# A layer norm taken chunk by chunk, and a K/V loop that empties its banks with two engines

## The reference

```python
n = layernorm(x)                                # no scale, no shift
Q, K, V = n @ Wq, n @ Wk, n @ Wv
Qf, Kf = elu(Q) + 1, elu(K) + 1                 # elu(z)+1 = max(z,0) + exp(min(z,0))
KV = einsum('lm,ln->mn', Kf, V); K1 = Kf.sum(0) # for each head
x = x + ((Qf @ KV) / (Qf @ K1 + eps)) @ Wo      # linear attention
y = layernorm(x)
y = y + mla(rmsnorm(y))                         # causal softmax attention, latent of 512
x = x + y + moe(rmsnorm(y))                     # 8 experts, top 2, hidden 2048 (all computed)
```

## Time and profile before

| | us |
|---|---|
| median of 3 runs | 3589.64 (3584.74 to 3591.18) |
| the profiled execution, its time | 3570.58 |
| its span, slowest core (core 6) | 3568.7 |
| spans of all cores | 3548.9 to 3568.7 |
| TensorE matmul busy | 2762.1 (77% of the span) |
| VectorE, ScalarE, POOL busy | 819.2, 721.4, 364.5 |
| mean granted TensorE clock, all cores | 0.886 to 0.889 |

### The profile page before, as it was taken

How to read it: one execution, slowest core, us unless ns; L and a number is a source line. 1 busy time by engine, 2 the same in 40 slices (tenths; PEclk the granted TensorE clock), 3 DMA queues, 4 the chain that set the end, 5 groups by cost and what they waited for, 6 DMA issues and landing times.

```text
span 3568.7 us, 36830 instructions; the slowest of 8 cores (3548.9 to 3568.7 us)
## 1 busy us (share of the span) xinstructions
PE 2762.1 (77%) x13813; PEld 1240.7 (35%) x14080; DVE 819.2 (23%) x1585; ACT 721.4 (20%) x809; POOL 364.5 (10%) x375
## 2 busy tenths in 40 slices
PE   1678554894555666657999989999999899999997
PEld 1333221442222222223444434444444344444443
DVE  4325444355333232230110011001101110011011
ACT  2001100103352535632001101110111011101110
POOL 0113100000101000002001101110111011101110
PEclk9888776895666767878999999999999999999999
DMA  8001003001000000009246443652464536525641
GB/s 180 1 1 26 0 1 48 1 4 21 1 1 0 1 1 1 1 1 104 24 51 71 42 66 35 71 62 23 57 71 37 70 36 71 59 22 61 71 80 51
DMA packets 297853, 135.97 MB, mean 38 GB/s; under 512 B 268880, under 2 KB 269904, under 8 KB 297680
## 3 DMA queue, kind: packets, MB, share of 16 engines
q0 software_dynamic: 292432, 116.69, 28.3%
q1 hardware_dynamic: 5248, 16.91, 1.5%
HBM read 241.73 MB, written 8.39 MB: 70 GB/s over the span
## 4 chain that ended last, share of the span: by engine, by line
PE 66%; DVE 14%; ACT 6%; issue 5%; DMA 5%; another core or an unknown queue 1%; DVEq 1%; ACTq 0%; POOL 0%; SPq 0%; POOLq 0%
PE PS L966 24%; PE PSQ L938 22%; ACT PTb L727 5%; PE PSQ L287 4%; DMA WSb<-w 3%; PE PSQ L716 3%; DVE PTb L737 3%; DVE accT L976 3%; PE PSQ L398 2%; PE PST L202 2%; PE PS L699 2%; PE PS L786 2%; PE PSQ L353 2%; PE PSQ L557 2%; DMA accT<-x 1%
## 5 line engine op out<-in xcount | busy, mean ns | idle before, releaser
L938 PE MATMUL PSQ<-N,WSb 128*128 128x512 bf16 x4013 | 897.2, 383 | 42.6 <-DMA WSb<-w 37.1
L966 PE MATMUL PS<-N 128*128 128x512 bf16 x2758 | 624.1, 379 | 63.8 <-DVE accT L976 61.0
L976 DVE SCALAR_TENSOR_TENSOR accT<-PS,gts,accT 128x512 f32<-128x512 f32 x256 | 192.1, 751 | 1739.2 <-PE PS L966 1693.6
L938 PEld LDWEIGHTS PSQ<-N,WSb 128*128 128x128 bf16 x4096 | 403.5, 99 | 533.5 <-issue 60.7
L947 ACT ACTIVATE N<-PSQ 128x1024 bf16<-128x1024 f32 x256 | 261.9, 1023 | 1604.7 <-PE PSQ L938 1604.7
L966 PEld LDWEIGHTS PS<-N 128*128 128x128 bf16 x2816 | 270.5, 98 | 408.6 <-issue 92.6
L727 ACT ACTIVATE PTb<-PSQ 128x1024 bf16<-128x1024 f32 x320 | 327.4, 1023 | 225.1 <-PE PSQ L716 209.7
L151 POOL DMA_DIRECT2D WSb<-w x256 | 223.8, 874 | 1209.3 <-PE PSQ L938 1206.1
L966 PE MATMUL PS<-A,N 128*128 128x512 bf16 x1257 | 287.6, 379 | 37.4 <-DVE accT L976 36.2
L699 PE MATMUL PS<-N,PTb 128*128 128x65 bf16 x2176 | 146.7, 218 | 212.5 <-DVE PTb L737 158.4
L716 PE MATMUL PSQ<-qpad,N 128*128 128x512 bf16 x587 | 244.4, 523 | 12.7 <-issue 7.9
(11 more groups left out here) (128 smaller groups left out, 1206.1 us busy)
## 6 DMA issues: line engine op xcount, KB each, us to landing
WSb<-w POOLq DMA_DIRECT2D x256, 256.0 KB, 4.7
N<-w POOLq DMA_DIRECT2D x11, 2048.0 KB, 14.5
A<-w POOLq DMA_DIRECT2D x5, 2048.0 KB, 14.6
accT<-x SPq DMA_DIRECT2D x4, 2048.0 KB, 34.1
out<-accT SPq DMA_DIRECT2D x2, 4096.0 KB, 12.9
N<-aWk POOLq DMA_DIRECT2D x1, 2048.0 KB, 34.7
N<-aWv POOLq DMA_DIRECT2D x1, 2048.0 KB, 56.9
A<-aWq POOLq DMA_DIRECT2D x1, 2048.0 KB, 67.8
```

The lines of the kernel that those rows point to most:

```text
L938: st=(kc == 0), sp=(kc == KD - 1): e_.matmul(out=QB[bb], lhsT=w1slot[sl][:, kk * 128:(kk + 1) * 128], rhs=N1v[:, kk, g * 1024 + hf * 512:g ...
L966: st=(kh == 0), sp=(kh == KH - 1): e_.matmul(out=YEB[pp][:, 0:512], lhsT=N2a[:, kk * 1024 + t_ * 128:kk * 1024 + t_ * 128 + 128], rhs=w2a[ ...
L976: tst = b.emit("v", lambda e_, pp=pair[half], d=dstp, tt_=qt, ee=e: e_.scalar_tensor_tensor(out=d, in0=YEB[pp][:, 0:512], scalar=gts.ap()[ ...
```

## The change

Two places are changed. In the layer norm the three loops over 16 tiles become one loop over the four chunks of x: sums and squares of four tiles, the small instructions on 4 columns of `st`, then normalisation and transposition of those four tiles. The fourth tile of a chunk is transposed and copied behind the first normalisation of the next chunk. In the K/V loop max and min are taken by halves of 512 columns (one bank each), the copy of V goes from VectorE to ScalarE, ahead of the exponent, and the banks' tokens follow: bank 0 is free after the first min, bank 1 after the second, banks 2 and 3 after ScalarE's copy. VectorE's wait for POOL's addition of the round before (`scr_guard[0]`) now stands ahead of the first max.

```diff
-    tsq = None
-    for t in range(NT):
-        acc_t = accT.ap()[:, t * 1024:(t + 1) * 1024]
-        b.wait("v", tok_xc[t // 4])
-        b.wait("s", tok_xc[t // 4])
...
     pend_tr = None
-    for t in range(NT):
...
+    for c in range(4):
+        lo = 4 * c
+        b.wait("v", tok_xc[c])
+        b.wait("s", tok_xc[c])
+        tsq = None
+        for t in range(lo, lo + 4):
+            acc_t = accT.ap()[:, t * 1024:(t + 1) * 1024]
+            b.emit("v", lambda e, a=acc_t, tt=t: e.reduce_sum(out=st[:, 16 + tt:17 + tt], in_=a, axis=AX.X))
+            tsq = b.emit("s", lambda e, a=acc_t, tt=t: e.activation(
+                out=scrF.ap(), in_=a, func=AF.Square, accum_out=st[:, 32 + tt:33 + tt]), inc="s")
+        b.wait("v", tsq)
+        b.emit("v", lambda e, l=lo: e.tensor_scalar_mul(out=st[:, 16 + l:20 + l], in0=st[:, 16 + l:20 + l], scalar1=1.0 / 1024))
...
+        b.wait("s", tv)
+        tsd = b.emit("s", lambda e, l=lo: e.activation(out=st[:, 32 + l:36 + l], in_=st[:, 32 + l:36 + l], func=AF.Sqrt, bias=EPS_LN), inc="s")
+        b.wait("v", tsd)
+        b.emit("v", lambda e, l=lo: e.reciprocal(out=st[:, 32 + l:36 + l], in_=st[:, 32 + l:36 + l]))
+        for t in range(lo, lo + 4):
...
+            b.wait("v", slot_guard[t % 2])
+            ta = b.emit("v", lambda e, a=acc_t, sl=slot, tt=t: e.tensor_scalar(
+                out=sl, in0=a, scalar1=st[:, 16 + tt:17 + tt], scalar2=st[:, 32 + tt:33 + tt],
+                op0=ALU.subtract, op1=ALU.mult), inc="v")
+            if pend_tr is not None:
+                ev, mm = transpose_tile(*pend_tr[0:3])
...
         b.wait("v", kf_slot_free[sl])
-        b.wait("v", v_slot_free[sl])
         kpsum = PSQ.ap()[:, 0:1024]
-        b.emit("v", lambda e, kp=kpsum, d=kf: e.tensor_scalar_max(out=d, in0=kp, scalar1=0.0))
         b.wait("v", scr_guard[0])
-        tmin = b.emit("v", lambda e, kp=kpsum: e.tensor_scalar_min(out=scrF.ap(), in0=kp, scalar1=0.0), inc="v")
+        b.emit("v", lambda e, kp=kpsum, d=kf: e.tensor_scalar_max(out=d[:, 0:512], in0=kp[:, 0:512], scalar1=0.0))
+        tmin0 = b.emit("v", lambda e, kp=kpsum: e.tensor_scalar_min(out=scrF.ap()[:, 0:512], in0=kp[:, 0:512], scalar1=0.0), inc="v")
+        b.emit("v", lambda e, kp=kpsum, d=kf: e.tensor_scalar_max(out=d[:, 512:1024], in0=kp[:, 512:1024], scalar1=0.0))
+        tmin = b.emit("v", lambda e, kp=kpsum: e.tensor_scalar_min(out=scrF.ap()[:, 512:1024], in0=kp[:, 512:1024], scalar1=0.0), inc="v")
+        vdst = vp.rearrange("p (h c) -> p h c", c=65)[:, :, 0:64]
+        vsrc = PSQ.ap()[:, 1024:2048].rearrange("p (h c) -> p h c", c=64)
+        b.wait("s", tok_kv)
+        b.wait("s", v_slot_free[sl])
+        tv = b.emit("s", lambda e, d=vdst, s_=vsrc: e.activation(out=d, in_=s_, func=AF.Copy), inc="s")
         b.wait("s", tmin)
         b.wait("s", scr_guard[0])
         te = b.emit("s", lambda e: e.activation(out=scrF.ap(), in_=scrF.ap(), func=AF.Exp), inc="s")
-        vdst = vp.rearrange("p (h c) -> p h c", c=65)[:, :, 0:64]
-        vsrc = PSQ.ap()[:, 1024:2048].rearrange("p (h c) -> p h c", c=64)
-        tv = b.emit("v", lambda e, d=vdst, s_=vsrc: e.tensor_copy(out=d, in_=s_), inc="v")
-        bank_free[0] = bank_free[1] = tmin
+        bank_free[0] = tmin0
+        bank_free[1] = tmin
         bank_free[2] = bank_free[3] = tv
         b.wait("g", te)
-        b.wait("g", tv)
```

More of the change, by code:

```diff
@@ L236, in build @@
-    pend_tr = None
-    for t in range(NT):
[L238 to L247, removed]
+    pend_tr = None
@@ new lines, in build @@
+    for c in range(4):
[10 more added lines that the diff above has]
+        b.emit("v", lambda e, l=lo: e.tensor_scalar_mul(out=st[:, 16 + l:20 + l], in0=st[:, 16 + l:20 + l], scalar1=1.0 / 1024))
+        b.emit("v", lambda e, l=lo: e.tensor_scalar_mul(out=st[:, 32 + l:36 + l], in0=st[:, 32 + l:36 + l], scalar1=1.0 / 1024))
+        b.emit("v", lambda e, l=lo: e.tensor_mul(out=st[:, l:l + 4], in0=st[:, 16 + l:20 + l], in1=st[:, 16 + l:20 + l]))
+        tv = b.emit("v", lambda e, l=lo: e.tensor_sub(out=st[:, 32 + l:36 + l], in0=st[:, 32 + l:36 + l], in1=st[:, l:l + 4]), inc="v")
+        b.wait("s", tv)
[3 more added lines that the diff above has]
+        for t in range(lo, lo + 4):
+            acc_t = accT.ap()[:, t * 1024:(t + 1) * 1024]
+            slot = stg1.ap()[:, (t % 2) * 1024:(t % 2) * 1024 + 1024]
+            b.wait("v", slot_guard[t % 2])
[4 more added lines that the diff above has]
+                ev, mm = transpose_tile(*pend_tr[0:3])
+                slot_guard[pend_tr[3] % 2] = mm
+            pend_tr = (slot, N1v[:, 0:8, t * 128:(t + 1) * 128], [ta], t)
```

## The result

The changed kernel took 3551.26 us (median of 10 runs) beside 3587.63 us for the kernel before (10 runs): 36.4 us less, ratio 0.9897 with a 95% interval of 0.9876 to 0.9919. The forecast was 3554 us, 35.3 us less.

What follows compares the result with a forecast made beforehand. The prediction took the kernel as mostly TensorE-bound, with gains possible only at the start and in the K/V loop. 18.5 + 11.8 + 5 = 35.3 us off 3589.6 gave 3554 us, range 3540 to 3573.

Steps and rivals of the forecast that it cites:

- The start: Program start to first projection matmul: layer norm by chunks brings that matmul to 80.0 instead of 98.47, 18.5 us less.
- More than 18.5 isn't there: Layer norm at the start: upper bound of 18.5 us on the gain, because VectorE's queue is full.
- The weights: DMA at the start: Wv still lands near 59.9 us, 19 us before it is wanted, despite the moved normalisations.
- Rival C: Start: weights stand still under the moved VectorE work, so the time is 3590 us, no change; chance 0.03.
- The loop's wait: K/V loop: TensorE restarts 3.24 instead of 4.04 us after the first max, 12.0 us in 15 restarts, 11.8 with the tail.
- rival E: K/V loop: ScalarE's copy into steps of 65 is slow and TensorE waits for it, 3618 us at 7 us; chance 0.04.
- That bank 0 is given back early is worth nothing: K/V loop: early release of bank 0 gains nothing, as TensorE asks for all four banks before its first matmul.
- The clock: K/V loop: TensorE's bursts shorten with less idle time, 5 us less, between +14.6 and -25.4.
- 22% of 25.4: K/V loop: idle shrinks 22%, so that share of the 25.4 us from all bursts at 2.4 GHz, rounded down to 5.
- all like the last burst of 9.57 us: K/V loop: the clock term's bad bound, every TensorE burst as long as the last, 14.6 us more.
- rival D: K/V loop: the clock stays up throughout, gaining the whole 25.4 us, for a time of 3534 us; chance 0.11.
- Rival F: Expert stage: both gains are given back where TensorE already waits for weights, time 3590 us; chance 0.04.

Runs made afterwards that it cites:

- e1: Kernel before with only the layer norm by chunks, its K/V loop unchanged; ratio 0.9957 to the kernel before.
- e6: Changed kernel with ScalarE instead of VectorE copying the layer norm's transposed tiles out of PSUM; ratio 0.9931 to the kernel before.
- e10: Changed kernel with max/min unsplit, K matmuls before V, and layer-norm tiles alternating between two banks, copied by VectorE and ScalarE; ratio 0.9747 to the kernel before.
- e4: Changed kernel with only the order of VectorE's and TensorE's waits in the K/V loop altered; ratio 0.9929 to the kernel before.
- e8: Changed kernel with ScalarE's V copy issued twice in each K/V round; ratio 0.9898 to the kernel before.
- e3: Changed kernel with max and min taken on 1024 columns again, V copy still on ScalarE; ratio 0.9875 to the kernel before.
- e2: Kernel before with only the K/V loop changed, its layer norm unchanged; ratio 0.9963 to the kernel before.
- e12: The changed kernel itself, unaltered, run again on another chip; ratio 0.9889 to the kernel before.
- e9_dummy_mm: Changed kernel with six unread matmuls added behind the K/V products of each round but the last; ratio 0.9845 to the kernel before.

## Why the prediction was right, step by step

**The start: right in mechanism, a term too dear** (18.5 forecast, 19.6 measured, 19.7 alone in e1). The walk through VectorE's queue holds: no wait for x behind 15 us, a chunk of 14.87 instead of 15.4. From its first reduction to the first projection matmul the forecast has 80.0 - 15.20 = 64.8 us; the 8 cores took 62.3 to 62.7. The mis-sized term is the round of small instructions, which the queue holds four times: I priced it at 2.34 us, and 48.94 to 50.73 is 1.79. Most of the difference is a pause that the kernel before has between its first two instructions (line below, its core 6) and no chunk of the changed kernel has; why it is gone isn't known. "More than 18.5 isn't there" was therefore wrong.

```profile
62.91 0.17 DVE L229 TENSOR_SCALAR stats<-stats 128x16 f32<-128x16 f32 x1 [0.54 <-DVE stats L228]
```

That the means came within 1.1 us hides part of this: I worked on core 6, which got its last chunk at 56.91, 2.0 us later than the cores' mean, and on core 6 the gain is 98.47 - 77.50 = 21.0. The bound of the stage is not VectorE alone, either: it waits 0.41 us for TensorE in most tiles, and e6 relieved VectorE of the copies and gained nothing, since one bank binds transposition and copy together. Only e10, with a second bank and both engines, got ahead; which of the two did it wasn't separated.

**The weights: right.** Wv lands 53.7 us after its issue, with the normalisations moved under it, 54.8 without. Rival C is refuted here. What holds for DMAs that POOL issues while VectorE normalises isn't tested, since all were issued by 8 us and the first normalisation starts behind 21 us.

**The loop's wait: right mechanism, size off.** The step "TensorE restarts after the last min, 3.24 instead of 4.04" measured 3.33 from the first max, and VectorE starts 0.08 us later still: 0.63 us a round, not 0.80, and only 0.3 in the first (4.21 to 3.88), together 9.1 in 15, not 12.0. TensorE's idle time on this wait is 45.5 us, not 43. The tail behind the last burst grew by 0.46 us instead of 0.25 (301.03 to 307.50 before, 266.02 to 272.95 on core 2). The 0.17 us are two waits already met that stand behind the one that comes last, which I priced at nothing: VectorE's for POOL, and TensorE's for ScalarE's token. e4 removed both by order alone. ScalarE's copy has 2.15 us of slack in the timeline, and a second one, 1.03 us more, delays no restart (e8): rival E is refuted. "That bank 0 is given back early is worth nothing" fits e3, and I ought to have drawn the consequence: the split then only costs.

**The clock: size and reasoning wrong, the sign not clear.** Forecast 5 us, measured 3.3. But five profiles have this same loop, and their bursts took 136.1, 136.9 (e2), 137.9 (e12), 138.9 (e6) and 139.8 us (e8; 136.6 without cores 6 and 7), beside 139.4 and 139.6 (e1) for the loop before. So the gain is 0 to 3 us and not clear of chance. The step that failed is the proportion, "22% of 25.4". The runs give the burst total over idle time in a round:

| kernel | idle before a burst, us | 16 bursts, us |
|---|---|---|
| before | 3.58 | 139.4 |
| changed, and the same loop in e2, e12, e6, e8 | 2.94 | 136.1 to 139.8 |
| e4_wait_order | 2.77 | 139.1 |
| e3_unsplit | 2.42 | 118.7 |
| e9_dummy_mm | 1.54 | 115.8 |

It isn't proportional: little or nothing down to 2.77, then most of it by 2.42. The first three rows lie closer together than single cores do. Of the changed kernel, single cores lay between 130.6 and 145.9. Nor does one idle gap decide. On core 2 of the changed kernel TensorE was idle equally long before these bursts:

```profile
146.61 9.92 PE L289 MATMUL PSQ<-N 128*128 128x512 bf16 x32 [2.94 <-DVE scrF L305]
...
160.11 10.00 PE L289 MATMUL PSQ<-N 128*128 128x512 bf16 x32 [2.95 <-DVE scrF L305]
...
197.94 7.07 PE L289 MATMUL PSQ<-N 128*128 128x512 bf16 x32 [2.95 <-DVE scrF L305]
...
208.59 7.07 PE L289 MATMUL PSQ<-N 128*128 128x512 bf16 x32 [2.95 <-DVE scrF L305]
```

What changed is the mixture. Bursts of 7.07 us went from 3 of 16 to 5.4 on the cores' mean, but long ones stayed at 5 and became longer: up to 10.02 us, where 9.73 was the longest before. So the sign that I had named, fewer than five bursts of 9.4 to 9.7 us, did not come (core 2 has six over 9.5), and "all like the last burst of 9.57 us" was no bound. The rule named beside rival D (the Trainium skill, TensorE: Matmul & The Clock Gate, "Why this matters for your kernels") lets the clock drop when a gap between bursts is too long and stay up otherwise. The trace doesn't bear that out for a single gap: at the same 2.94 us bursts came at full speed and not, and rival D's 25.4 us did not come. The 0.69 in the long stretch of short waits stands against it too.

**The sum.** Up to the Q projection's start the forecast was 35.3 and the cores' mean gave 31.4; the medians of the times gave 36.4, and the ratio's interval stands for 29 to 44. That 3554 came so close to 3551 is partly luck: the stages miss by +1.1 at the start, -3.3 in the wait with its tail and -1.7 in the clock, together -3.9, and the rest is the spread of the runs. Rival F (given back later) is refuted by the stages behind the Q projection, 3251.8 and 3250.4 us.

## What to carry to other kernels

When an evacuation stands between two bursts of TensorE, moving it to another engine takes off tenths; issuing the matmuls so that one half of the banks is emptied under the other half's matmuls takes off the whole wait and the half-speed time behind it (here 69 us on top of the 12 of the change, 26 of them from taking back the split). Splitting an instruction by bank can pay only if the consumer's first wait is by bank too; here it cost. A wait that is already met is not free behind the one that comes last (0.08 and 0.10 us here). And a few tenths of idle time less may change nothing at TensorE's clock or much, so judge such edits by bursts and idle time together, over several executions: one profile of this loop says 3.3 us of gain, another none.

## What was not expected of the hardware

- 0.17 us less idle time in each round did not shorten the bursts (e4: 139.1 us beside 136.1 to 139.8), and 0.5 us less took 17 us off them (e3).
- At the same idle time of 2.94 us on the same core, bursts last 7.07 us in some rounds and 10.00 in others.
- With TensorE busy almost without a pause, two of eight cores of one execution were granted 0.81 through the K/V stage (8.58 us a burst) while others had 1.00 (7.07).
- A wait that has long been met costs 0.08 us on VectorE and 0.10 us on TensorE when it stands last (0.32 and 0.25 us in the changed kernel, 0.25 and 0.15 in e4).
